# A Mamba block between two expert layers: three groups of the second routing worked inside the turns, and the second expert layer begun before the last turn's output

## The reference

```python
x = x + 0.5 * _L0_ffn_ref(_layernorm(x), router_w, w1, w2)
x = x + _L0_attn_ref(_layernorm(x), ...)      # the Mamba block, which adds its own input once more
x = x + 0.5 * _L0_ffn_ref(_layernorm(x), router_w, w1, w2)
```

## Time and profile before

| what | us |
|---|---|
| median of 3 runs | 1088.42 |
| lowest and highest run | 1088.01, 1103.92 |
| the profiled execution, its own time | 1089.27 |
| span of its trace, first to last instruction | 1087.40 |
| PE, DVE, ACT, POOL busy in the span | 902.4, 881.8, 726.4, 573.4 |

### The profile page before, as it was taken

One profiled execution on the slowest core, in us unless ns is written; L12 is line 12 of the kernel. 1 busy time (PEld: TensorE's weight loads), 2 busy tenths in 40 slices (PEclk: granted clock), 3 DMA queues, 4 the chain that ended last, 5 costly groups with the idle time before them and its releaser, 6 DMA issues.

```text
span 1087.4 us, 40975 instructions
## 1 busy us (share of the span) xinstructions
PE 902.4 (83%) x14616; PEld 773.4 (71%) x14616; DVE 881.8 (81%) x2802; ACT 726.4 (67%) x1741; POOL 573.4 (53%) x644
## 2 busy tenths in 40 slices
PE   2228899999989899898999998998942888999990
PEld 1117888998967677676777776876632777889990
DVE  6998884575589899899899998998878788855785
ACT  3454655566679799798899998997633555556650
POOL 4764675566444444445444554443357455755641
PEclk9999999999989999999999999999965889999996
DMA  9944578585346677577676676764522454665997
GB/s 255 303 135 94 128 155 189 102 176 107 88 90 128 113 133 129 109 130 127 118 131 121 130 130 120 130 118 85 96 61 91 100 116 116 146 149 105 192 229 246
DMA packets 186965, 147.44 MB, mean 136 GB/s; under 512 B 106480, under 2 KB 154608, under 8 KB 186640
## 3 DMA queue, kind: packets, MB, share of 16 engines
q0 software_dynamic: 42672, 70.19, 32.1%
q1 hardware_dynamic: 138336, 69.38, 28.6%
q10 hardware_dynamic: 5760, 5.26, 1.7%
HBM read 41.35 MB, written 51.22 MB: 85 GB/s over the span
## 4 chain that ended last, share of the span: by engine, by line
DVE 40%; PE 32%; issue 11%; DMA 5%; SPq 4%; ACT 3%; POOL 3%; DVEq 0%; POOLq 0%; ACTq 0%
PE bank L926 12%; PE bank L939 11%; DVE lake L1213 7%; DVE arena L1267 4%; PE bank L1629 2%; PE bank L1698 2%; POOL disp L753 2%; DVE q_ L1190 2%; SPq L830 2%; DVE lake L1220 2%; ACT lake L1495 2%; DVE lake L1274 2%; DVE lake L1246 2%; DVE lake L1234 2%; DVE arena L1044 1%
## 5 line engine op out<-in xcount | busy, mean ns | idle before, releaser
L926 PE MATMUL bank<-arena,weights 128*128 128x128 f16 x3408 | 221.7, 223 | 15.2 <-DMA arena<-disp 12.9
L871 POOL DMA_INDIRECT ychosen<-arena,didx x142 | 150.9, 1063 | 147.8 <-issue 84.6
L926 PEld LDWEIGHTS bank<-arena,weights 128*128 x3408 | 207.7, 100 | 20.4 <-issue 17.5
L939 PE MATMUL bank<-weights,arena 128*128 x1704 | 212.5, 276 | 10.4 <-DVE arena L1049 9.3
L939 PEld LDWEIGHTS bank<-weights,arena 128*128 128x128 f16 x1704 | 162.5, 99 | 30.1 <-issue 12.3
L980 ACT ACTIVATE arena<-bank 128x512 f32<-128x512 f32 x142 | 84.6, 596 | 134.8 <-PE bank L926 114.7
L1044 DVE TENSOR_TENSOR arena<-arena 128x512 f32<-128x512 f32 x142 | 98.3, 692 | 94.1 <-ACT arena L980 88.7
L753 POOL DMA_INDIRECT disp<-lake,sloti x128 | 133.7, 1045 | 46.6 <-issue 37.5
L1213 DVE SCALAR_TENSOR_TENSOR lake<-lake,vec 128x128 f32<-128x128 f32 x480 | 128.7, 346 | 0.0
L1355 POOL DMA_DIRECT2D lake<-turned_y x32 | 27.8, 869 | 153.8 <-DMA turned_y<-lake 153.8
L1049 DVE TENSOR_TENSOR arena<-arena 128x512 f16<-128x512 f32 x142 | 98.2, 692 | 4.9
(11 more groups left out here) (195 smaller groups left out, 1966.1 us busy)
## 6 DMA issues: line engine op xcount, KB each, us to landing
arena<-in_w SPq DMA_DIRECT2D x16, 512.0 KB, 9.6
yg<-ychosen SPq DMA_DIRECT2D x32, 256.0 KB, 2.9
X<-yg POOLq DMA_DIRECT2D x64, 128.0 KB, 3.6
arena<-lake SPq DMA_DIRECT2D x128, 64.0 KB, 3.3
lake<-lake POOLq DMA_DIRECT2D x32, 256.0 KB, 3.3
turned_y<-lake SPq DMA_DIRECT2D x128, 64.0 KB, 1.9
lake<-turned_y POOLq DMA_DIRECT2D x32, 256.0 KB, 4.1
lake<-ychosen SPq DMA_DIRECT2D x32, 256.0 KB, 4.8
```

What stands on the lines that cost most here:

```text
L871: pool.indirect_dma_start(ychosen, bass.IndirectOffsetOnAxis(ap=didx[:, place:place + 1], axis=0), ysb[n % YB][:, :], None).then_inc(S(f"y ...
L926: mm = pe.matmul(o, chunk(where, 2 * ("hl".index(w) * WN + c * HID + m * P), P), v, start=c == 0 and n_ == 0, stop=c == KD - 1 and n_ == 2)
L939: mm = pe.matmul(down_ps(n), x, chunk(where, 2 * ((2 + "hl".index(w)) * WN + c * D), D), start=c == 0 and n_ == 0, stop=c == KH - 1 and n_ ...
```

## The change

With `EG = 3`, the first three groups of the second routing (12 blocks, `AHEAD`) are taken out of the routing generator and worked inside the turns, one block in two turns. A block k has its statistics and power in turn 2k+2, its norm, high and low half in turn 2k+3, its turning and logits in turn 2k+4. A group's choice stands in the turn 9 behind its first, the one-hot and the ranks one later, the placing in the next, the weights in the next. The rows lie in a ring of six buffers (`rows16`) in space that the experts use, and POOL scatters a block's two copies at the end of a turn (`row_send`): turns 13 to 16, 21 to 24, and two blocks each in turns 29 and 30. In turn 31 DVE computes the first table, then two groups' statistics (now groups 3 and 4); the routing generator starts at group 3. To make room, the gate product `gz` has one buffer instead of two, and `GT` and `xo` lie elsewhere. The bodies of choice, placing, weights and table become functions that both paths call, unchanged in what they issue.

Each engine but POOL and SP enters the second expert layer one step earlier: PE issues the up products of tiles 0 and 1, ACT their relus, DVE the low half of tile 0, before the turned gate and the output product of block 31. The routing of group 3 follows behind these, then tile 2. SP loads tile 0 once the table is there, all scatters of the turns have landed and the last intra-block product is done.

```diff
+EG, RING = 3, 6
+AHEAD = EG * GT_
+ROW_TURN = 2
 TILES = (2 * NT * P + E * (P - 1)) // P
...
+def row_step(i, lag):
+
+    n = i - ROW_TURN - lag
+    return n // 2 if n % 2 == 0 and 0 <= n // 2 < AHEAD else None
+
+
+def group_step(i, lag):
+
+    n = i - ROW_TURN - lag
+    return n // (2 * GT_) if n % (2 * GT_) == 0 and 0 <= n // (2 * GT_) < EG else None
+
+
+def rows_leaving(i):
+
+    turn = {k: 2 * GT_ * (k // GT_) + 11 + (k % GT_ if k < AHEAD - GT_ else k % GT_ // 2) for k in range(AHEAD)}
+    return [k for k in range(AHEAD) if turn[k] == i - ROW_TURN]
 
...
         used[0] = 0
         R = carve(NH * QT)
         bd = carve(NH * B * HP)
+        row32 = [carve(ROW // 2) for p in range(RING)]
+        rows16 = [t.bitcast(F16) for t in row32]
+        assert used[0] <= experts_end - D - DI
+        used[0] = experts_end - D - DI
         GT = carve(DI)
...
                         sp.wait_ge(S("stage_used"), XTH_FREE)
+                    if r and s == 0:
+                        sp.wait_ge(S("m_intra"), NT)
...
-                 {3: ("ranks", 4), 4: ("turned", 5), 5: ("logits", 5), 10: ("ranks", 5), 11: ("turned", 6), 12: ("logits", 6),
+                 {1: ("ranks", 3), 2: ("logits", 4), 3: ("ranks", 4), 4: ("turned", 5), 5: ("logits", 5), 10: ("ranks", 5), 11: ("turned", 6), 12: ("logits", 6),
...
-            until(routing, ("logits", 4) if r else ("turned", 5))
+            if r == 0:
+                until(routing, ("turned", 5))
...
+                if r and s - 1 == 1:
+                    until(turns, None)
                 if s - 1 in PE_AT[r]:
                     until(routing, PE_AT[r][s - 1])
...
                     yout(s - 2)
+                if r and s == 1:
+                    until(turns, None)
...
-            until(routing, ("place", 3) if r else ("split",))
+            if r == 0:
+                until(routing, ("split",))
...
                     take(s - 1)
+                if r and s == 0:
+                    until(turns, None)
...
+            def row_stats(k):
+                if k == 0:
+                    start_count(dve)
+                dve.wait_ge(S("m_xout"), 16 * (k + 1))
+                chain.link(dve.bn_stats(st[:, 0:6], Xk(k)))
+                chain.link(dve.bn_aggr(row(mv, k, 2), st[:, 0:6]))
+                dve.tensor_scalar(row(var, k, 1), row(mv, k, 2)[:, 1:2], EPS, None, ALU.add).then_inc(S("var"), 1)
+
+            def row_norm(k):
+                dve.wait_ge(S("rstd"), NG + k + 1)
+                dve.tensor_scalar(row_xh[:, :], Xk(k), row(mv, k, 2)[:, 0:1], row(rstd, k, 1), ALU.subtract, ALU.mult)\
+                    .then_inc(S("xh"), 1)
+
+            def row_low(k):
+                d = rows16[k % RING]
+                dve.wait_ge(S("hi"), 2 * NG + k + 1)
+                dve.tensor_tensor(d[:, D:2 * D], row_xh[:, :], d[:, 0:D], ALU.subtract).then_inc(S("lo"), 1)
...
                     decays(i, 1)
+                if row_step(i, 0) is not None:
+                    row_stats(row_step(i, 0))
+                if row_step(i, 1) is not None:
+                    row_norm(row_step(i, 1))
+                if group_step(i, 9) is not None:
+                    row_choose(group_step(i, 9), i)
+                if group_step(i, 10) is not None:
+                    row_one_hot(group_step(i, 10))
+                if group_step(i, 11) is not None:
+                    row_places(group_step(i, 11), i)
+                if group_step(i, 12) is not None:
+                    row_weights(group_step(i, 12))
+                if inside(i):
                     decays(i, 2)
                 if inside(i - 1):
                     gate(i - 1)
...
                 if i == NT - 1:
-                    until(routing, ("stats", 1))
+                    until(table(dve, chain, 1, 0), None)
+                    until(routing, ("stats", EG + 1))
                 if inside(i):
                     gate_in(i)
+                if row_step(i, 1) is not None:
+                    row_low(row_step(i, 1))
                 if inside(i + 1):
...
-                    until(routing, ("place", 0))
+                    until(routing, ("stats", EG + 2))
...
+            def row_send(k):
+                g, j = k // GT_, k % GT_
+                pool.wait_ge(S("slot"), NG + g + 1)
+                pool.wait_ge(S("lo"), 2 * NG + k + 1)
+                pool.wait_ge(S("tok"), NG + k + 1)
+                hold(pool, "pool")
+                for x in range(2):
+                    pool.indirect_dma_start(disp, bass.IndirectOffsetOnAxis(ap=row_slots[g][:, 2 * j + x:2 * j + x + 1], axis=0),
+                                            rows16[k % RING][:, :], None).then_inc(S(f"row_out_{k % RING}"), 16)
+
             for i in range(FIRST, LAST):
...
+                for k in rows_leaving(i):
+                    row_send(k)
...
+            def row_high(k):
+                d = rows16[k % RING]
+                if k == 0:
+                    all_stored(act, TILES)
+                after(act, f"row_out_{k % RING}", 32 * (k // RING))
+                act.activation(row32[k % RING][:, D:D + 2], const(C_TOK)[:, 2 * k:2 * k + 2], ACT.Copy).then_inc(S("tok"), 1)
+                act.wait_ge(S("xh"), 2 * NG + k + 1)
+                act.activation(d[:, 0:D], row_xh[:, :], ACT.Copy).then_inc(S("hi"), 1)
+
+            def row_turned(k):
+                act.wait_ge(S("xt_ps"), 2 * NG + k + 1)
+                act.wait_ge(S("logit_ps"), 2 * NG + k)
+                act.activation(row_xT[:, :], row_xt_ps, ACT.Copy).then_inc(S("xt"), 1)
+
+            def row_ratio(g):
+                act.wait_ge(S("dm"), NG + g + 1)
+                act.activation(ed[g % 2][:, :], dm[g % 2][:, :], ACT.Exp, scale=1.0 / WSCALE).then_inc(S("ed"), 1)
...
-                    until(routing, ("ratio", 0))
+                    until(routing, ("rows", EG))
...
+            def row_turned(k, turn):
+                pe.wait_ge(S("lo"), 2 * NG + k + 1)
+                pe.wait_ge(S("m_hn"), turn + 1)
+                for c in range(2 * KD):
+                    m = pe.transpose(row_xt_ps[:, c * P:(c + 1) * P], rows16[k % RING][:, c * P:(c + 1) * P], ident16)
+                m.then_inc(S("xt_ps"), 1)
+
...
+            def row_logits(k, turn):
+                pe.wait_ge(S("xt"), 2 * NG + k + 1)
+                bank_free(turn)
+                j = k % GT_
+                for c in range(2 * KD):
+                    m = pe.matmul(row_logit_ps[:, j * 2 * E:(j + 1) * 2 * E], row_xT[:, c * P:(c + 1) * P],
+                                  rwf[:, c % KD * 2 * E:(c % KD + 1) * 2 * E], start=c == 0, stop=c == 2 * KD - 1)
+                m.then_inc(S("logit_ps"), 1)
...
                     gate_in(i)
+                if row_step(i, 2) is not None:
+                    row_turned(row_step(i, 2), i)
...
+                if row_step(i, 2) is not None:
+                    row_logits(row_step(i, 2), i)
+                if group_step(i, 10) is not None:
+                    row_ranks(group_step(i, 10), i)
+                if group_step(i, 9) is not None:
+                    pe.wait_ge(S("dm"), NG + group_step(i, 9) + 1)
+                if group_step(i, 11) is not None:
+                    pe.wait_ge(S("slot"), NG + group_step(i, 11) + 1)
...
-                    until(routing, ("ranks", 0))
...
-            until(turns, None)
...
+            until(turns, ("last",))
```

More of the change, by code:

```diff
@@ L548, in route_dve @@
-            start_count()
-            dve.memset(taken[:, :], 0.0)
-            stats(0)
-            stats(1)
-            yield ("stats", 1)
+                dve.wait_ge(S("ed"), n0 + g + 1)
+                softmax(dve, chain, g)
+            first = EG if r else 0
+            if r == 0:
+                start_count(dve)
+            stats(first)
+            stats(first + 1)
+            yield ("stats", first + 1)
             if r:
                 dve.wait_ge(S("m_intra"), NT)
-            norm(0)
@@ L556, in route_dve @@
-            low(0)
-            for g in range(NG):
-                ahead = g == 0 or (r == 0 and g == HG)
+            norm(first)
+            low(first)
+            for g in range(first, NG):
+                ahead = g == first or (r == 0 and g == HG)
                 if g + 2 < (NG if r else HG + 2):
@@ L593, in route_dve @@
                     if groups == g + 1:
-                        yield from table(i)
+                        yield from table(dve, chain, r, i)
             weights_of(NG - 1)
@@ L652, in route_act, with counts @@
                     yield ("halved",)
+        def counts(pe, o, to):
+            for j in range(GT_):
+                for i in range(j):
+                    pe.matmul(to[:, j * E:(j + 1) * E], ones16, row(o, i, E), start=i == 0, stop=False)
+                pe.matmul(to[:, j * E:(j + 1) * E], before16, row(o, j, E), start=j == 0, stop=True)
+            for j in range(GT_):
+                m = pe.matmul(to[:, GT_ * E:(GT_ + 1) * E], ones16, row(o, j, E), start=j == 0, stop=j == GT_ - 1)
```

(17 more changed lines are left out.)

418 lines of the change are left out of this document (244 added, 174 removed).

## The result

The changed kernel takes 1097.97 us (median of 20 runs, 1089.19 to 1109.22) against 1089.68 us for the kernel before in the same session (20 runs, 1077.52 to 1103.92). The ratio is 1.0078 with a 95% interval of 1.0056 to 1.01: slower by about 0.8%, some 8 us. The forecast was 1086 us, a gain of 2.5 us. The time lies in the range given, on the wrong side. The profiled execution took 1092.98 us with a span of 1091.2; the one of before 1089.27 with 1087.4.

What follows compares the result with a forecast made beforehand. DVE was taken to bound a plain turn and the routing list behind the turns. 1089.27 + 29 (work in the turns) - 31.5 (saved behind them) = 1086.8 us, 1086 on the median's footing; range 1075 to 1099.

Steps and rivals of the forecast that it cites:

- The stops: PE's five stops of about 2.4 us in the turns: one more or less, 2 to 4 us either way.
- The work in the turns: Added row and group work, nearly all on DVE, lengthens the turn stretch by 29 us, bounds 22 to 42.
- Behind the turns: Last turn and start of the experts: group 4 is placed at 833.8 against 865.27, 31.5 us saved.
- the rank product's 0.7: Between last gate and group 3's placing: the rank product takes 0.7 us, no longer covered by a low part.
- that allowance: From group 3's to group 4's placing: 2.4 us for PE serving ranks and relus later than DVE asks.
- After group 4: From group 4's placing on, all engines' order and work stay as before, so the difference carries to the end.
- B: Rival, in the turns: POOL's powers block DVE, 8.8 us more, 1095 us; chance 0.20.
- C: Rival, in the turns: the new work is swallowed by DVE's waits, 16.6 us less, 1069 us; chance 0.08.
- D: Rival, experts' start: PE leads, third up product right behind group 3's ranks, 37.9 us saved, 1080 us; chance 0.15.
- E: Rival, experts' start: POOL leads with group 3's scatters, only 24.6 us saved, 1093 us; chance 0.12.

Runs made afterwards that it cites:

- e2: The changed kernel with 18 instructions that do nothing put once into PE's stream ahead of the turns: 1083.27 us, ratio 0.9959 to the kernel before.
- e5: The changed kernel with 10 to 18 small f32 filler matmuls in every third turn, ahead of its last products: 1071.02 us, ratio 0.9869 to the kernel before.
- e8: As e5, with the filler moved ahead of the turned gate and the last two turns covered too: 1065.71 us, ratio 0.9824 to the kernel before.
- e7: As e5, but PE, ACT and DVE finish the last turns before the second expert layer's first up products and relus: 1074.57 us, ratio 0.9894.
- e10: The changed kernel with 43 small f32 matmuls put once ahead of the second turn's turned gate: 1082.7 us, ratio 0.9922 to the kernel before.
- e6: The kernel before with small f32 filler matmuls (17 in one turn, 12 in six) ahead of the turn's last products: 1069.97 us, ratio 0.9847.
- e9: As e6, the kernel before with filler, but placed ahead of the turned gate: 1069.36 us, ratio 0.9865 to the kernel before.

## Why the prediction was wrong, point by point

**The stops: the step that failed.** The prediction said of PE's five stops that they "may be one more or less: 2 to 4 us either way in each case". I had priced their number as noise and left it out of the sum. It is set by the count of PE's instructions, which the change alters: ten stops for five. Summed as each stopped turn's length over that of a like turn without a stop, they cost about 31 us after the change and 17 before, 3.1 and 3.4 each, more than the stop itself (2.1 and 2.4), because the tanh and DVE's L1301 come late after it. That is 14 of the 15 us between 44.1 and 29. e2 takes some of them away with 18 idle instructions and is 13 us faster; e5 and e8 take nearly all away, and some 30 come back.

**The work in the turns: right, 1 to 2 us too small.** Even row turns are 15.2 to 15.4 us long and odd ones 14.8 to 14.9, against 14.46: +0.8 to +0.9 and +0.35 to +0.4, as forecast. The turn with the third group's one-hot and ranks alone takes 16.76 (+2.3), within the 2.5 forecast. But where a one-hot and a block's statistics share a turn, in turns 12 and 20, it takes 17.7 to 19.2 and 18.2 to 18.7 us in the five profiles without a stop there (e2, e5, e7, e8, e10), 3.2 to 4.7 and 3.8 to 4.2 over 14.47, where 0.8 and 2.3 give 3.1. In turn 12 of e5 DVE waits 1.5 us for the tanh and 0.8 for the filler; I had allowed for neither. e5 less e6 leaves 30.4 for my 29.

**Behind the turns: right mechanism, 3.1 us too small up to group 4.** From the opening of the list to group 4's weights it took 865.27 - 784.46 = 80.8 us before and takes 872.22 - 826.04 = 46.2: 34.6 saved where I said 31.5. The gate comes 16.0 us after the opening (forecast 16.3). From there to group 3's placing I took 15.0 + 0.7 from the old rows; it was 13.0. PE's turned gate takes 0.66 us where it took 1.11 and the output product 3.32 where it took 3.78, now that up products stand right ahead of them; e7, where they don't, has 1.12 and 3.50, and e5 0.66 and 1.99. And the rank product's 0.7 did not show. From 855.01 to 872.22 it took 17.2; I had 14.9 + 2.4 = 17.3, so that allowance, an estimate, came out.

**After group 4: a difference that is not the change's alone.** I carried the difference to the end. It grew by 3.1 us (from 222.1 to 219.0). From group 4's choice to the end the five profiles without the change take 228.7 to 234.4 us (the kernel before 231.8) and the seven with it 226.1 to 230.6 (the changed one 228.4), so one execution differs from the next by as much. In these two it can be seen in the rows. Busy time by window of the first 22 us from there (PE, PEld, DVE, ACT, POOL, granted clock, DMA), before and after:

```profile
865.50:888.00 22.50, 19.10 (x245) 17.32 (x244) 20.66 (x80) 11.09 (x23) 12.90 (x13) 0.88 0.51 115
```
```profile
872.70:895.00 22.30, 18.93 (x278) 17.50 (x276) 20.45 (x80) 12.41 (x26) 12.89 (x13) 1.00 0.37 97
```

With the same idle time of 2.70 us ahead of the rank product, the kernel before ran the next up and down product in 2.74 and 2.77 us, at the clock's lower level (1.2 GHz), the changed one in 1.51 and 1.47 at the full 2.4. The time from one group's logits to the next's fell from 27.06 to 24.22 us. Why the clock fell in one and not in the other the rows don't say.

**The rivals.** B (POOL's powers block DVE) fell: DVE's L1348 has a median of 684 ns as before and a maximum of 715, L1333 one of 751, and all their rows over 700 ns are three, 0.13 us too long together, where B had 8.8. L1509's twelve powers run up to 843 ns beside a shortest of 542, so it is POOL that is held up, as with L1324. C (the work is swallowed) fell with 44.1. D had the third up product right behind group 3's ranks, and so it stands (854.11, ranks from 853.27); but the list of DVE behind it took 17.2 us, about the 17.3 that I had, so this lead bought nothing by itself. E had POOL's scatters hold the tiles up: they begin at 856.00, 1 us behind the placing, and behind group 4 PE waits for DVE and ACT, not for POOL. The measured 1098 lies nearest B's 1095, for none of B's reasons; that it lies in my range at all is luck, since the range was drawn for B with one stop more, and five more came.

## What to carry to other kernels

Where an engine's timeline shows idle time that nothing explains, find out what recurs: the place in the program, the period in turns, the count of instructions between two of them. Such stops, as here, can belong to the layout of the program and not to the noise, and an edit elsewhere that adds nine slots a turn can double them. So when two versions of a loop with very short matmuls are compared, shift each by a few instructions that do nothing, or better fill both until no boundary falls where instructions run fastest; otherwise the comparison is one of layouts.

## What the hardware showed that I had not expected

- PE's program arrives in pieces of 16 KB, 122 in this kernel. If a piece ends late in 128 matmuls that take 1.3 us or right behind them (matmul 99 to 135), PE stops for up to 2.8 us in three cases of four, until 1.2 to 1.6 us after the end of the piece's packet.
- An instruction that only holds waits already met costs PE 85 ns (72 in 6.1 us). A small f32 matmul (32x32 by 32x16), four slots, costs some 40 ns: 18 of them held DVE up by 0.8 us ahead of the last products, and by up to 0.7 ahead of the turned gate.
- Whether the stops also make the scatter of the runs is not shown. Six runs of e6 lie within 2.9 us (1068.22 to 1071.1) and six of e9 within 6.2, but six of e8, which has no stop either, within 10.7; twenty of the kernel before are spread over 26.4 us.
